# Projection, value, turn-out and output side work of the first attention, divided into halves behind two units in a row

## The chip, the cores and the metric

The kernel runs on one core of one Trainium2 chip. The metric is device time in microseconds (us) of one execution, and the number compared is the median of several runs. A core has five engines that run their own instruction lists side by side and meet at semaphores: TensorE (PE in the profile, with its weight loads as PEld), VectorE (DVE), ScalarE (ACT), GpSimd (POOL) and SyncE (SP), which here issues DMAs.

## The reference, cut to what matters

The input x has shape (4, 512, 256). Four stages add to it in turn: a cross-attention of 16 heads of 64 over a context with a mask, a mixture of experts with 8 experts, a banded self-query attention, and a second mixture of experts. The change touches the first stage alone:

```
Qh = (layernorm(x) @ Wq).reshape(n, t, 16, 64)      # Wq, Wk, Wv: 256 x 1024
Kh = (ctx @ Wk).reshape(n, t, 16, 64)
Vh = (ctx @ Wv).reshape(n, t, 16, 64)
energy = einsum('nqhd,nkhd->nhqk', Qh, Kh) / 8
energy = where(mask == 0, -1e20, energy)
heads_out = einsum('nhqk,nkhd->nqhd', softmax(energy), Vh)
x = x + heads_out.reshape(n, t, 1024) @ Wo          # Wo: 1024 x 256
```

## The kernel before, in words

Every float32 matrix is held as two float16 parts, hi and lo, and a product is made of three matmuls (`three_products`, L197 to L199).

The first attention runs over 32 groups, numbered g = 0 to 31: 4 batches of 8 pairs of heads. A group has 8 units, numbered j = 0 to 7: two heads times four blocks of 128 queries. A unit u is a row of steps on several engines, and TensorE takes them with lags: in its step u it makes the scores of unit u (`score`, L427 and L428, into one of two banks `sc`), transposes the exponentials of unit u-3 (`turn`, L435, into `et`) and multiplies the values of unit u-5 (`attend`, twelve small matmuls into `ob`). VectorE does the masking and the minimum of unit u (L540, L542), then the lo part of unit u-3 (L518). ScalarE does the hi part of unit u-3 (L484), then the exponential of unit u (L491).

Behind its step u TensorE does a piece of side work, which `side_work(g, j)` names. In the kernel before these are whole pieces:

- j = 0: `k`, six matmuls of 512 columns, the keys of group g+1;
- j = 1: `q`, six such matmuls, the queries of group g+1;
- j = 4: `v`, six such matmuls, values of the next batch (batches 0 to 2 only, so groups 0 to 23);
- j = 5: `w`, 24 matmuls of 256 columns, an output projection of the batch before (in groups 9 to 12, 17 to 20 and 25 to 28);
- j = 7: `t`, four transposes of the normalised output of group g-1.

All of them write into one of two PSUM banks `pj`, taken in turn. `open_group` makes the first matmul of a piece wait until the piece two before it has been taken out of its bank: by ScalarE (`copy`, L478, semaphore `copied`) or, for `w`, by VectorE (`add_out`, L514, semaphore `added`). ScalarE does the copy of a piece of step u-1 as the last thing of its step u, and VectorE does `add_out` of a `w` of step u-1 behind its L518 of step u.

After the copy GpSimd splits the piece into hi and lo (`split`, L333 and L335; for k and q into `nat_k` and `nat_q`), in the order in which the pieces are finished. In twelve groups (0 to 3, 8 to 11, 16 to 19) it also turns a block of the mask into a bias (`bias`, L310) between q and v. SyncE then moves the keys and queries to the layout of the scores with DMAs (`stack(g+1)`: four of `kk`, L288, four of `qq`, L292), and behind these it loads the next mask block (L279). The first score of group g+1 waits until the `kk` and `qq` of its first head have landed, the first two of each four (semaphore `stacked[0]`).

Of the kernel before, what the change touches and what calls it, by code (L numbers as in the profile page):

```python
# [17 lines left out]
B, S, D = 4, 512, 256  # L18
NT = B * S // P
QT = S // P  # L20
DT = D // P
# [3 lines left out]
CT = CW // P  # L25
PAIRS = HEADS // 2
# [175 lines left out]
def side_work(g, j):  # L202


    p, b = g % PAIRS, g // PAIRS
    if j == 0 and g + 1 < PAIRS0:
        return "k", g + 1
    if j == 1 and g + 1 < PAIRS0:
        return "q", g + 1
    if j == 4 and b + 1 < B:  # L210
        return "v", (b + 1, p)
    if j == 5 and b >= 1 and 1 <= p <= QT:
        return "w", (b - 1, p - 1)
    if j == 7 and g >= 1:
        return "t", g - 1
    return None


def number_groups():

    groups, copies, adds = {}, {}, {}
    order = [("k", 0), ("q", 0)] + [("v", (0, n)) for n in range(V_GROUPS)]
    order += [side_work(g, j) for g in range(PAIRS0) for j in range(UNITS) if side_work(g, j) is not None]
# [11 lines left out]
def phase_attention0(nc, sem, T, dram):  # L235
# [3 lines left out]
    with ExitStack() as ctx:  # L239
# [32 lines left out]
        with nc.Block() as block:  # L272
# [31 lines left out]
            @block.gpsimd  # L304
            def _(pool):
                def bias(n):
                    pool.wait_ge(mask_in[n % 2], 16 * (n // 2 + 1))
                    if n >= 2 * QT:
                        pool.wait_ge(masked_ok, (n // QT - 1) * PAIRS * UNITS)
                    pool.tensor_scalar(mask_bias[n // QT % 2][:, n % QT, :], mask_raw[n % 2][:], 0.0, MASKED, ALU.is_equal, ALU.mult).then_inc(bias_ok, 1)  # L310

                def split(what):
                    kind, at = what
                    n = COPY0[what]
                    src = raw[n % NRAW][:]
                    pool.wait_ge(copied, n + 1)
                    if kind == "v":
                        b, part = at
                        if b >= 2:
                            pool.wait_ge(pv_done, (b - 1) * PAIRS * UNITS)  # L320
                        hi, lo = v_part(v[b % 2].hi, part), v_part(v[b % 2].lo, part)
                        src = src.rearrange("p (h d) -> p h d", d=DK)
                    elif kind == "t":
                        b, ct = at // PAIRS, at % PAIRS
                        if b >= 2:
                            pool.wait_ge(pj_full, GROUP0["w", (b - 2, QT - 1)] + 1)
                        hi, lo = o_t[b % 2].hi[:, ct, :], o_t[b % 2].lo[:, ct, :]
# [12 lines left out]
                bias(0)  # L340
                bias(1)
                split(("k", 0))
                split(("q", 0))
                bias(2)
                bias(3)
                for n in range(V_GROUPS):
                    split(("v", (0, n)))
                for g in range(PAIRS0):
                    for j in range(UNITS):
                        what = side_work(g, j)  # L350
                        if what in COPY0:
                            split(what)
                        if j == 2 and g // PAIRS + 1 < B and g % PAIRS < QT:
                            bias((g // PAIRS + 1) * QT + g % PAIRS)
                split(("t", PAIRS0 - 1))

            @block.tensor
            def _(pe):
# [7 lines left out]
                            pe.wait_ge(added, ADD0[before] + 1)  # L366
                    return pj[n % 2]

                def project(what, w, src_t):

                    out = open_group(what)
                    b, col = what[1] // PAIRS, (what[1] % PAIRS) * P
                    for c in range(DT):
                        mm = three_products(pe, out[:], (w.hi[:, c, col:col + P], w.lo[:, c, col:col + P]),
                                            (src_t.hi[:, c, b * S:(b + 1) * S], src_t.lo[:, c, b * S:(b + 1) * S]),
                                            c == 0, c == DT - 1)
                    mm.then_inc(pj_full, 1)

                def project_v(what):
# [3 lines left out]
                    out = open_group(what)  # L383
                    for c in range(DT):
                        mm = three_products(pe, out[:], (T.ctx_t.hi[:, c, rows], T.ctx_t.lo[:, c, rows]),
                                            (T.wv0.hi[:, c, cols], T.wv0.lo[:, c, cols]), c == 0, c == DT - 1)
                    mm.then_inc(pj_full, 1)

                def turn_out(what):
                    g = what[1]  # L390
# [6 lines left out]
                def project_out(what):  # L397
                    b, qt = what[1]
                    out = open_group(what)
                    pe.wait_ge(split_done, COPY0["t", (b + 1) * PAIRS - 1] + 1)  # L400
                    cols = slice(qt * P, (qt + 1) * P)
                    for ct in range(CT):
                        mm = three_products(pe, out[:, 0:D], (o_t[b % 2].hi[:, ct, cols], o_t[b % 2].lo[:, ct, cols]),
                                            (T.wo0.hi[:, ct, :], T.wo0.lo[:, ct, :]), ct == 0, ct == CT - 1)
                    mm.then_inc(pj_full, 1)

                def do_side_work(what):
                    if what[0] == "k":
                        project(what, T.wk0, T.ctx_t)
                    elif what[0] == "q":  # L410
                        project(what, T.wq0, T.z_t)
                    elif what[0] == "v":
                        project_v(what)
                    elif what[0] == "t":
                        turn_out(what)
                    else:
                        project_out(what)

                def score(u):
                    g, j = u // UNITS, u % UNITS  # L420
# [30 lines left out]
                project(("k", 0), T.wk0, T.ctx_t)  # L451
                project(("q", 0), T.wq0, T.z_t)
                for n in range(V_GROUPS):
                    project_v(("v", (0, n)))
                pe.wait_ge(v_const, 4)
                units = PAIRS0 * UNITS
                for u in range(units + ATTEND_LAG):
                    if u < units:
                        score(u)
                    if 0 <= u - TURN_LAG < units:  # L460
                        turn(u - TURN_LAG)
                    if u >= ATTEND_LAG:
                        attend(u - ATTEND_LAG)
                    what = side_work(u // UNITS, u % UNITS) if u < units else None
                    if what is not None:
                        do_side_work(what)
                turn_out(("t", PAIRS0 - 1))
                for qt in range(QT):
                    project_out(("w", (B - 1, qt)))

            @block.scalar
            def _(act):
# [25 lines left out]
                for u in range(units + TURN_LAG):  # L498
                    if u >= TURN_LAG:
                        turned_part(u - TURN_LAG)  # L500
                    if u < units:
                        exponent(u)
                    what = side_work((u - 1) // UNITS, (u - 1) % UNITS) if 1 <= u <= units else None
                    if what in COPY0:
                        copy(what)
                copy(("t", PAIRS0 - 1))

            @block.vector
            def _(dve):
# [36 lines left out]
                for u in range(units + TURN_LAG):  # L546
# [1351 lines left out]
```

## Time and profile before

| | us |
|---|---|
| runs | 1392.19, 1393.86, 1393.17; median 1393.17 |
| profiled execution, its own time | 1389.44 |
| its span, first to last instruction | 1387.7 |
| TensorE, matmuls | 1127.9 busy (81%) |
| VectorE | 799.5 (58%) |
| ScalarE | 626.4 (45%) |
| GpSimd | 507.8 (37%) |
| granted TensorE clock over the span | 0.905 |

The first attention fills the span from about 72 us (first score) to 573 us. Busy time of matmuls counts each from its start to its modelled end, and neighbours overlap. So the pace of TensorE is read from start to start: two score matmuls of a unit start 0.21 to 0.22 us apart though each is listed with 0.38. A timeline row gives the start, the duration, the engine, the line, the operation, and at its end, in brackets, the idle time of the engine before it with what released it. A row of the windows view gives the stretch, its length, the busy time (and in parentheses the number of instructions) of PE, PEld, DVE, ACT and POOL, then the granted clock as a share of 2.4 GHz, the busy share of the DMA engines and GB/s.

### The profile page before, as it was taken

How to read it: one execution, taken by the hardware profiler on the slowest of the kernel's cores; microseconds unless marked ns; L12 is line 12 of the kernel's file. 1: busy time of each engine (PE TensorE's matmuls, PEld its weight loads, DVE VectorE, ACT ScalarE, POOL GpSimd, SP SyncE). 2: the span in 40 equal slices, each digit the busy share in tenths (PEclk: the TensorE clock that was granted, in tenths of full speed). 3: DMA queues.
4: the chain of work that ended last, by engine and by line, in shares of the span. 5: the costliest groups of instructions: out<-in, count | busy, mean ns of one | idle time of the engine just before them, and what ended most of it. 6: DMA issues, size and time to landing. Idle time of an engine off the chain costs nothing. (4 is left out here: it accounts for less than half of the span.)

```text
span 1387.7 us, 29963 instructions
## 1 busy us (share of the span) xinstructions
PE 1127.9 (81%) x10895; PEld 856.4 (62%) x10896; DVE 799.5 (58%) x2325; ACT 626.4 (45%) x1171; POOL 507.8 (37%) x491
## 2 busy tenths in 40 slices
PE   2499999999999999454799916558899953699997
PEld 1166777777777776353588812335666633588886
DVE  7267787787778778546511134356677751255553
ACT  3277787787778778010022113125455530333331
POOL 2666545444544332210325332189820003011112
PEclk9899999999999999655599967979999985799998
DMA  6122222222222121430146342545521141111110
GB/s 242 53 62 62 70 55 63 55 70 62 63 50 67 48 50 44 151 124 1 31 129 204 108 113 88 178 130 165 161 64 44 33 127 65 47 32 27 26 23 9
DMA packets 80222, 110.94 MB, mean 80 GB/s; under 512 B 11552, under 2 KB 58400, under 8 KB 79712
## 3 DMA queue, kind: packets, MB, share of 16 engines
q1 hardware_dynamic: 69632, 88.23, 21.6%
q0 software_dynamic: 10464, 21.01, 6.4%
q8 instruction: 81, 1.33, 0.4%
q14 instruction: 45, 0.37, 0.1%
HBM read 59.86 MB, written 24.70 MB: 61 GB/s over the span
## 5 line engine op out<-in xcount | busy, mean ns | idle before, releaser
L542 DVE CUSTOM_DVE_ANT_0 masked<-sc,mask_bias 128x512 f32<-128x512 f32 x256 | 175.5, 686 | 57.7 <-issue 39.3
L518 DVE TENSOR_TENSOR e_t_lo<-et,e_t_hi 128x512 f16<-128x512 f32 x256 | 176.6, 690 | 49.9 <-ACT e_t_hi L484 47.6
L491 ACT ACTIVATE e<-masked,neg_max 128x512 f32<-128x512 f32 x256 | 184.3, 720 | 26.9 <-DVE neg_max L542 26.4
L484 ACT ACTIVATE e_t_hi<-et 128x512 f16<-128x512 f32 x256 | 152.1, 594 | 88.1 <-PE et L435 87.8
L435 PEld LDWEIGHTS et<-ident,e 128*128 128x128 f32 x1024 | 125.7, 141 | 54.1 <-ACT e L491 6.3
L435 PE MATMUL et<-ident,e 128*128 128x128 f32 x1024 | 154.1, 273 | 1.4 <-ACT e L491 0.7
L1266 ACT ACTIVATE d_e<-d_st 128x384 f32<-128x384 f32 (+1 forms) x192 | 98.0, 529 | 113.4 <-PE d_st L1351 98.1
L197 PE MATMUL ob<-v_hi,e_t_hi 128*128 128x65 f16 x1024 | 119.0, 193 | 0.6 <-DVE e_t_lo L518 0.6
L198 PE MATMUL ob<-v_lo,e_t_hi 128*128 128x65 f16 x1024 | 119.2, 193 | 0.0
L199 PE MATMUL ob<-v_hi,e_t_lo 128*128 128x65 f16 x1024 | 118.4, 193 | 0.0
L427 PE MATMUL sc<-kk,qq 128*128 128x512 f16 x256 | 96.9, 379 | 5.2 <-DMA qq<-nat_q 4.8
L197 PE MATMUL h_hb<-h_xt_hi,experts_hi 128*128 128x256 f16 x352 | 97.1, 276 | 4.3 <-DVE h_xt_lo L1732 3.9
L198 PE MATMUL h_hb<-h_xt_lo,experts_hi 128*128 128x256 f16 x352 | 97.0, 276 | 0.0
L199 PE MATMUL h_hb<-h_xt_hi,experts_lo 128*128 128x256 f16 x352 | 97.0, 275 | 0.0
L428 PE MATMUL sc<-kk,qq 128*128 128x512 f16 x256 | 96.9, 379 | 0.0
L198 PEld LDWEIGHTS ob<-v_lo,e_t_hi 128*128 128x128 f16 x1024 | 94.5, 97 | 2.9
L197 PEld LDWEIGHTS ob<-v_hi,e_t_hi 128*128 128x128 f16 x1024 | 95.7, 97 | 0.8 <-DVE e_t_lo L518 0.7
L1703 POOL DMA_INDIRECT out<-h_res,h_token x22 | 34.2, 1553 | 166.8 <-DVE h_res L1755 161.5
L199 PEld LDWEIGHTS ob<-v_hi,e_t_lo 128*128 128x128 f16 x1024 | 94.7, 97 | 0.0
L1346 PE MATMUL d_wk<-d_k,d_q 128*128 128x384 f16 (+1 forms) x256 | 72.4, 310 | 26.2 <-DMA d_q<-d_k 22.7
L478 ACT ACTIVATE raw<-pj 128x512 f32<-128x512 f32 x128 | 75.0, 586 | 32.0 <-POOL v_lo L335 15.9
L1278 DVE TENSOR_REDUCE d_mx<-d_wk 128x1 f32<-128x384 f32 x128 | 66.9, 553 | 35.0 <-PE d_wk L1351 28.7
(315 smaller groups left out, 2902.2 us busy)
## 6 DMA issues: line engine op xcount, KB each, us to landing
kk<-nat_k SPq DMA_DIRECT2D x128, 128.0 KB, 2.3
raw<-in_fc SPq DMA_DIRECT2D x16, 1024.0 KB, 6.7
qq<-nat_q SPq DMA_DIRECT2D x128, 64.0 KB, 2.0
mask_raw<-in_mask SPq DMA_DIRECT2D x16, 256.0 KB, 2.9
scratch_stack<-c_qk_hi SPq DMA_DIRECT2D x32, 128.0 KB
scratch_stack<-c_qk_lo SPq DMA_DIRECT2D x32, 128.0 KB
d_expert_raw<-in_gate_w POOLq DMA_DIRECT2D x8, 512.0 KB, 4.1
d_expert_raw<-in_up_w POOLq DMA_DIRECT2D x8, 512.0 KB, 4.0
```

Of the source, the lines that this page charges most:

```text
L197: pe.matmul(out, stat[0], mov[0], start=first, stop=False)
L198: pe.matmul(out, stat[0], mov[1], start=False, stop=False)
L199: return pe.matmul(out, stat[1], mov[0], start=False, stop=last)
L427: pe.matmul(sc[j % 2][:], stat, kk[g % 2][:, a, 0, :], start=True, stop=False)
L428: pe.matmul(sc[j % 2][:], stat, kk[g % 2][:, a, 1, :], start=False, stop=True).then_inc(scores, 1)
L435: mm = pe.transpose(et[u % 2][:, kt, :], e[u % NBUF][:, kt * P:(kt + 1) * P], T.ident[:])
L478: nc.scalar.activation(raw[n % NRAW][:], pj[GROUP0[what] % 2][:], ACT.Copy).then_inc(copied, 1)
L484: nc.scalar.activation(e_t[u % NBUF].hi[:], et[u % 2][:], ACT.Copy).then_inc(turned_hi, 1)
L491: nc.scalar.activation(e[u % NBUF][:], masked[u % NBUF][:], ACT.Exp, bias=neg_max[:, g % 2, j:j + 1], scale=-1.0).then_inc(exp_ok, 1)
L518: nc.vector.tensor_tensor(e_t[u % NBUF].lo[:], et[u % 2][:], e_t[u % NBUF].hi[:], ALU.subtract).then_inc(turned_lo, 1)
L542: nc.vector.tensor_tensor_reduce(masked[u % NBUF][:], sc[j % 2][:], mask_bias[g // PAIRS % 2][:, j % QT, :], -SCALE0, 3e38, ALU.add, ALU.m ...
L1266: nc.scalar.activation(part(e[m % EBUF][:, 2 * half + i // 3, :, :], i % 3), src, ACT.Exp, scale=SCALE1).then_inc(exp_ok, 1)
```

## The change: what it does, and the diff

`side_work` now returns a list of halves. The keys stand behind units 0 and 1, the queries behind 2 and 3, the values behind 4 and 5, the output projection behind 6 and 7, and the turn-out stays behind 7. A half of k, q or v is three matmuls; a half of w is twelve. Both halves add into the same bank, only the first half opens it, and only the second half reports it full. A new function `complete(u)` lists the pieces that end behind unit u, and ScalarE, VectorE and GpSimd follow it: they take a piece out one step after its second half. Matmuls, copies, splits and DMAs are the same in number and size.

```diff
     p, b = g % PAIRS, g // PAIRS
-    if j == 0 and g + 1 < PAIRS0:
-        return "k", g + 1
-    if j == 1 and g + 1 < PAIRS0:
-        return "q", g + 1
-    if j == 4 and b + 1 < B:
-        return "v", (b + 1, p)
-    if j == 5 and b >= 1 and 1 <= p <= QT:
-        return "w", (b - 1, p - 1)
+    parts = []
+    if j < 2 and g + 1 < PAIRS0:
+        parts.append((("k", g + 1), j))
+    if 2 <= j < 4 and g + 1 < PAIRS0:
+        parts.append((("q", g + 1), j - 2))
+    if 4 <= j < 6 and b + 1 < B:
+        parts.append((("v", (b + 1, p)), j - 4))
+    if j >= 6 and b >= 1 and 1 <= p <= QT:
+        parts.append((("w", (b - 1, p - 1)), j - 6))
     if j == 7 and g >= 1:
-        return "t", g - 1
-    return None
+        parts.append((("t", g - 1), 1))
+    return parts
+
+
+def complete(u):
+
+    return [what for what, half in side_work(u // UNITS, u % UNITS) if half == 1] if 0 <= u < PAIRS0 * UNITS else []
...
# POOL: the order of the splits, and the place of the mask bias
-                        if j == 2 and g // PAIRS + 1 < B and g % PAIRS < QT:
+                        if j == 4 and g // PAIRS + 1 < B and g % PAIRS < QT:
                             bias((g // PAIRS + 1) * QT + g % PAIRS)
...
# PE: one half of a projection (project_v and project_out alike)
-                def project(what, w, src_t):
+                def project(what, w, src_t, halves):
 
-                    out = open_group(what)
+                    out = open_group(what) if 0 in halves else pj[GROUP0[what] % 2]
                     b, col = what[1] // PAIRS, (what[1] % PAIRS) * P
-                    for c in range(DT):
+                    for c in halves:
...
-                    mm.then_inc(pj_full, 1)
+                    if 1 in halves:
+                        mm.then_inc(pj_full, 1)
...
# ACT
-                    what = side_work((u - 1) // UNITS, (u - 1) % UNITS) if 1 <= u <= units else None
-                    if what in COPY0:
-                        copy(what)
+                    for what in complete(u - 1):
+                        if what in COPY0:
+                            copy(what)
...
# DVE
-                        what = side_work((u - 1) // UNITS, (u - 1) % UNITS) if u >= 1 else None
-                        if what in ADD0:
-                            add_out(what)
+                        for what in complete(u - 1):
+                            if what in ADD0:
+                                add_out(what)
```

The instruction lists of GpSimd and SyncE keep their order. Two places on other engines move.

On ScalarE, in a group with v, from the copy of t to that of q, before: L484 is the hi part (`e_t_hi`), L491 the exponential (`e`), L478 the copy out of `pj`.

```order
L478 ACTIVATE raw<-pj 128x512 [waits split_done,pj_full]
L484 ACTIVATE e_t_hi<-et 128x512 [waits pv_done,turned]
L491 ACTIVATE e<-masked,neg_max 128x512 [waits turned,masked_ok]
L478 ACTIVATE raw<-pj 128x512 [waits split_done,pj_full]
L484 ACTIVATE e_t_hi<-et 128x512 [waits pv_done,turned]
L491 ACTIVATE e<-masked,neg_max 128x512 [waits turned,masked_ok]
L478 ACTIVATE raw<-pj 128x512 [waits split_done,pj_full]
```

In the changed kernel, from the copy of t to that of k (its L487, L493 and L500 are L478, L484 and L491 of before):

```order
L487 ACTIVATE raw<-pj 128x512 [waits split_done,pj_full]
L493 ACTIVATE e_t_hi<-et 128x512 [waits pv_done,turned]
L500 ACTIVATE e<-masked,neg_max 128x512 [waits turned,masked_ok]
L493 ACTIVATE e_t_hi<-et 128x512 [waits pv_done,turned]
L500 ACTIVATE e<-masked,neg_max 128x512 [waits turned,masked_ok]
L487 ACTIVATE raw<-pj 128x512 [waits split_done,pj_full]
```

Before, the copies of t, k and q stood in three steps in a row (j = 0, 1, 2); now k's is two steps behind t's, and q's two behind k's, in step j = 4.

On VectorE in group 9, around the addition of the output projection (`x<-pj,x`), before; it stands between the lo part of step j = 6 and the masking of step j = 7, and behind it a whole step follows before TensorE opens the bank again:

```order
L527 RECIPROCAL rden<-ob 128x4 [waits normed,pv_done]
L529 TENSOR_TENSOR o<-ob,rden 128x4x64 [waits rden_ok]
L540 MEMSET gate 1x1 [waits exp_ok,scores]
L542 ISA masked,neg_max<-sc,mask_bias 128x512
L542 ISA neg_max 128x1
L518 TENSOR_TENSOR e_t_lo<-et,e_t_hi 128x512 [waits turned_hi]
L514 TENSOR_TENSOR x<-pj,x 128x256 [waits pj_full]
```

And in the changed kernel, where the addition stands in step j = 0 of group 10 (L523, L527, L551, L536 and L538 are L514, L518, L542, L527 and L529 of before):

```order
L549 MEMSET gate 1x1 [waits exp_ok,scores]
L551 ISA masked,neg_max<-sc,mask_bias 128x512
L551 ISA neg_max 128x1
L527 TENSOR_TENSOR e_t_lo<-et,e_t_hi 128x512 [waits turned_hi]
L523 TENSOR_TENSOR x<-pj,x 128x256 [waits pj_full]
L549 MEMSET gate 1x1 [waits exp_ok,scores]
L551 ISA masked,neg_max<-sc,mask_bias 128x512
L551 ISA neg_max 128x1
L527 TENSOR_TENSOR e_t_lo<-et,e_t_hi 128x512 [waits turned_hi]
L536 RECIPROCAL rden<-ob 128x4 [waits normed,pj_full,pv_done]
```

The addition moved two steps back, over the border of the group. The first matmul of k in step j = 0 is the one that waits for it (`added`), in both kernels.

## Rows read from the trace of the kernel before

**Rows 1.** Two stretches of the first attention, busy time by engine, from the windows view.
```profile
100.00:200.00 100.00, 97.19 (x1127) 70.45 (x1126) 78.26 (x243) 78.17 (x136) 54.53 (x59) 1.00 0.26 62
300.00:400.00 100.00, 100.00 (x1138) 74.85 (x1137) 73.67 (x230) 72.62 (x127) 52.40 (x56) 1.00 0.24 60
```

**Rows 2.** Waits from 72 to 560 us: engine, line, releaser, us, times, longest.
```profile
PE sc L427 <- DMA qq<-nat_q: 4.8, 4, 2.0
```

**Rows 3.** Timeline of TensorE in group 15: unit starts, q's first matmul, group 16.
```profile
297.67 0.38 PE L427 MATMUL sc<-kk,qq 128*128 128x512 f16 x1
...
300.19 0.38 PE L427 MATMUL sc<-kk,qq 128*128 128x512 f16 x1
...
301.42 0.38 PE L197 MATMUL pj<-z_t_hi,wq_hi 128*128 128x512 f16 x1
...
302.72 0.38 PE L427 MATMUL sc<-kk,qq 128*128 128x512 f16 x1
...
305.18 0.38 PE L427 MATMUL sc<-kk,qq 128*128 128x512 f16 x1
...
311.85 0.38 PE L427 MATMUL sc<-kk,qq 128*128 128x512 f16 x1
```

**Rows 4.** Timeline, the way of q(16) from its bank: copy, split, DMA issue.
```profile
304.89 0.59 ACT L478 ACTIVATE raw<-pj 128x512 f32<-128x512 f32 x1
...
306.24 1.16 POOL L335 TENSOR_TENSOR nat_q<-raw,nat_q 128x512 f16<-128x512 f32 x1
...
307.42 2.44 SPq L292 DMA_DIRECT2D qq<-nat_q  x4
```

**Rows 5.** Timeline of groups 3 and 4: SyncE, the delayed group start, GpSimd, SyncE again.
```profile
127.31 2.51 SPq L292 DMA_DIRECT2D qq<-nat_q  x4
129.87 0.58 SPq L279 DMA_DIRECT2D mask_raw<-in_mask  x1
129.99 0.39 PE L427 MATMUL sc<-kk,qq 128*128 128x512 f16 x1 [0.88 <-DMA qq<-nat_q]
...
132.76 1.94 POOL L310 TENSOR_SCALAR mask_bias<-mask_raw 128x512 bf16<-128x512 int32 x1 [6.12 <-DMA mask_raw<-in_mask]
...
142.52 2.53 SPq L292 DMA_DIRECT2D qq<-nat_q  x4
```

**Rows 6.** Timeline of group 18, step j = 6: score, lo part, addition.
```profile
356.76 0.38 PE L427 MATMUL sc<-kk,qq 128*128 128x512 f16 x1
...
358.46 0.69 DVE L518 TENSOR_TENSOR e_t_lo<-et,e_t_hi 128x512 f16<-128x512 f32 x1 [0.36 <-ACT e_t_hi L484]
...
359.07 0.41 DVE L514 TENSOR_TENSOR x<-pj,x 128x256 f32<-128x256 f32 x1
```

**Rows 7.** Timeline of TensorE: first scores of groups 24, 25, 29, 30, 31.
```profile
435.91 0.38 PE L427 MATMUL sc<-kk,qq 128*128 128x512 f16 x1
...
449.33 0.39 PE L427 MATMUL sc<-kk,qq 128*128 128x512 f16 x1 [0.20 <-DVE e_t_lo L518]
...
511.55 0.38 PE L427 MATMUL sc<-kk,qq 128*128 128x512 f16 x1
...
524.60 0.38 PE L427 MATMUL sc<-kk,qq 128*128 128x512 f16 x1
...
537.73 0.38 PE L427 MATMUL sc<-kk,qq 128*128 128x512 f16 x1
```

**Rows 8.** Timeline of SyncE in group 5: the second of the four issues of qq(6).
```profile
155.91 1.87 SPq L292 DMA_DIRECT2D qq<-nat_q  x1
```

**Rows 9.** Timeline of TensorE: first scores of groups 1 and 2.
```profile
85.08 0.39 PE L427 MATMUL sc<-kk,qq 128*128 128x512 f16 x1 [1.96 <-DMA qq<-nat_q]
...
99.28 0.38 PE L427 MATMUL sc<-kk,qq 128*128 128x512 f16 x1
```

**Rows 10.** Windows view: around the wait of group 1, and the end of the attention.
```profile
85.00:100.00 15.00, 14.92 (x171) 10.96 (x172) 10.99 (x36) 10.42 (x20) 7.06 (x7) 1.00 0.36 86
...
560.00:565.00 5.00, 5.00 (x26) 3.46 (x24) 0.26 (x1) 0.00 (x0) 0.00 (x0) 0.51 0.01 3
```

More of the change, by code:

```diff
@@ L222, in number_groups @@
     order = [("k", 0), ("q", 0)] + [("v", (0, n)) for n in range(V_GROUPS)]
-    order += [side_work(g, j) for g in range(PAIRS0) for j in range(UNITS) if side_work(g, j) is not None]
+    order += [what for u in range(PAIRS0 * UNITS) for what in complete(u)]
     order += [("t", PAIRS0 - 1)] + [("w", (B - 1, qt)) for qt in range(QT)]
@@ L349, in _ @@
                     for j in range(UNITS):
-                        what = side_work(g, j)
-                        if what in COPY0:
-                            split(what)
-                        if j == 2 and g // PAIRS + 1 < B and g % PAIRS < QT:
+                        for what in complete(g * UNITS + j):
+                            if what in COPY0:
+                                split(what)
+                        if j == 4 and g // PAIRS + 1 < B and g % PAIRS < QT:
                             bias((g // PAIRS + 1) * QT + g % PAIRS)
@@ L376, in project, with project_v @@
                                             c == 0, c == DT - 1)
-                    mm.then_inc(pj_full, 1)
-                def project_v(what):
+                    if 1 in halves:
+                        mm.then_inc(pj_full, 1)
+                def project_v(what, halves):
                     b, n = what[1]
@@ L382, in project_v @@
                     cols = slice((n % 2) * 512, (n % 2 + 1) * 512)
-                    out = open_group(what)
-                    for c in range(DT):
+                    out = open_group(what) if 0 in halves else pj[GROUP0[what] % 2]
+                    for c in halves:
                         mm = three_products(pe, out[:], (T.ctx_t.hi[:, c, rows], T.ctx_t.lo[:, c, rows]),
                                             (T.wv0.hi[:, c, cols], T.wv0.lo[:, c, cols]), c == 0, c == DT - 1)
-                    mm.then_inc(pj_full, 1)
+                    if 1 in halves:
+                        mm.then_inc(pj_full, 1)
                 def turn_out(what):
@@ L395, in turn_out, with project_out, do_side_work @@
                     mm.then_inc(pj_full, 1)
-                def project_out(what):
+                def project_out(what, halves):
                     b, qt = what[1]
-                    out = open_group(what)
+                    out = open_group(what) if 0 in halves else pj[GROUP0[what] % 2]
                     pe.wait_ge(split_done, COPY0["t", (b + 1) * PAIRS - 1] + 1)
                     cols = slice(qt * P, (qt + 1) * P)
-                    for ct in range(CT):
+                    for ct in [half * CT // 2 + i for half in halves for i in range(CT // 2)]:
                         mm = three_products(pe, out[:, 0:D], (o_t[b % 2].hi[:, ct, cols], o_t[b % 2].lo[:, ct, cols]),
                                             (T.wo0.hi[:, ct, :], T.wo0.lo[:, ct, :]), ct == 0, ct == CT - 1)
-                    mm.then_inc(pj_full, 1)
-                def do_side_work(what):
+                    if 1 in halves:
+                        mm.then_inc(pj_full, 1)
+                def do_side_work(what, half):
                     if what[0] == "k":
-                        project(what, T.wk0, T.ctx_t)
+                        project(what, T.wk0, T.ctx_t, [half])
                     elif what[0] == "q":
-                        project(what, T.wq0, T.z_t)
+                        project(what, T.wq0, T.z_t, [half])
                     elif what[0] == "v":
-                        project_v(what)
+                        project_v(what, [half])
                     elif what[0] == "t":
@@ L416, in do_side_work @@
                     else:
-                        project_out(what)
+                        project_out(what, [half])
                 def score(u):
@@ L449, in attend @@
                     mm.then_inc(pv_done, 1)
-                project(("k", 0), T.wk0, T.ctx_t)
-                project(("q", 0), T.wq0, T.z_t)
+                project(("k", 0), T.wk0, T.ctx_t, [0, 1])
+                project(("q", 0), T.wq0, T.z_t, [0, 1])
                 for n in range(V_GROUPS):
-                    project_v(("v", (0, n)))
+                    project_v(("v", (0, n)), [0, 1])
                 pe.wait_ge(v_const, 4)
@@ L463, in _ @@
                         attend(u - ATTEND_LAG)
-                    what = side_work(u // UNITS, u % UNITS) if u < units else None
-                    if what is not None:
-                        do_side_work(what)
+                    if u < units:
+                        for what, half in side_work(u // UNITS, u % UNITS):
+                            do_side_work(what, half)
                 turn_out(("t", PAIRS0 - 1))
                 for qt in range(QT):
-                    project_out(("w", (B - 1, qt)))
+                    project_out(("w", (B - 1, qt)), [0, 1])
             @block.scalar
@@ L502, in _ @@
                         exponent(u)
-                    what = side_work((u - 1) // UNITS, (u - 1) % UNITS) if 1 <= u <= units else None
-                    if what in COPY0:
-                        copy(what)
+                    for what in complete(u - 1):
+                        if what in COPY0:
+                            copy(what)
                 copy(("t", PAIRS0 - 1))
```

## The prediction

> **What bounds the kernel now.** I read the windows first. In the first attention TensorE is busy 97.19 of 100 us early on and 100.00 of 100 in the middle, at a granted clock of 1.00, while VectorE, ScalarE and GpSimd have 74 to 78, 73 to 78 and 52 to 55 [rows 1]. So TensorE sets the pace, and an engine with a quarter of its time free can only matter through a wait. The list of waits comes next: TensorE's matmuls wait longest for the `qq` DMAs, 4.8 us in four places of the whole stage [rows 2]. Side work moved about on an engine that never waits costs nothing and gains nothing; only waits that go or come count. To price these I took the starts of the score matmuls in the timeline, since a matmul's listed duration overlaps its neighbour's. Group 15 stands for the groups with k, q and v and no w: it runs from 297.67 to 311.85, which is 14.18 us. Its first unit (with k) takes 2.52 and its second (with q) 2.53, so q is complete at 302.72, 5.05 us into the group; four units have passed at 305.18, 7.51 us into it [rows 3].
>
> How much slack has each result of the side work? The way of q(16) is the longest: complete on TensorE at 302.72, copied by ScalarE at 304.89, split on GpSimd with the lo part from 306.24, and issued by SyncE at 307.42, that is 4.70 us after completion [rows 3, 4]. The copy starts 2.17 us late because it stands behind the exponential of the next step, which has to wait for that step's score. I looked at all 31 such ways: in 22 of them the time is 4.70 to 4.72 us, and in the nine others, which follow a mask block or the first values, it is longer. What an issue needs until the score may start is read where TensorE waited for it: issue at 127.31, score at 129.99, so 2.68 us [rows 5]. In group 15 there were 311.85 - 307.42 = 4.43 us, so q had 1.75 us to spare.
>
> **The change part by part.** The work is unchanged, instruction by instruction; every term is a wait.
>
> *Keys, queries and the start of the next group.* k ends one unit later and q two. The first four units hold the same matmuls as before, so q is complete 7.51 us into the group in place of 5.05: 2.46 us later, against 1.75 to spare. The ScalarE place of q's copy relative to the next step's score and exponential is the same as before, so I keep 4.70. The next group then can't start before 7.51 + 4.70 + 2.68 = 14.89 us: 0.71 us more than 14.18. GpSimd is free when q's copy comes, since k was split well before. This falls on each group that has v and no w and isn't already held by something else: 5 to 8, 13 to 16 and 21 to 23, eleven of them, 7.8 us. In the twelve groups 9 to 12, 17 to 20 and, with less room, 25 to 28, w makes the group 16.8 (15.55 in the last batch) us long, more than 14.89: nothing.
>
> *Last batch.* Without v the groups are shorter: group 24 takes 449.33 - 435.91 = 13.42, group 29 13.05, group 30 13.13 [rows 7]. Each becomes 14.89: 1.47 + 1.84 + 1.76 = 5.1 us. TensorE idles about 2 us in each. A wait of 1.96 us before group 1 left the granted clock at 1.00 in the 15 us behind it [rows 9, 10], so I add nothing for the clock.
>
> [...]
>
> *First batch.* Groups 1 to 4 hang on a ring of GpSimd and SyncE: the mask load is issued behind qq, the bias waits for it, v, t, k and q wait behind the bias on GpSimd, and the next qq waits for these. One turn is 142.52 - 127.31 = 15.21 us [rows 5], longer than 14.89, and the order on both engines is unchanged, so the ring keeps its pace. It only enters later: group 2 starts 0.71 us later than 85.08 + 14.20 = 99.28 [rows 9], and the first mask load with it. Between 0.7 and 1.4 us, since in groups 1 to 3 the time from the mask's issue to the bias varies by 0.7 us: I take 1.0. Group 1 itself is held by the splits of the first values, which the change doesn't touch: nothing.
>
> *Output projection and its bank.* This is the largest term. Pieces take the two banks in turn, in the order k, q, v, w, t; k of the next group so takes the bank of w. Before, w ended in step 5 and was added in step 6, two steps ahead of that k. Now it ends in step 7, and its addition stands behind VectorE's masking and lo part of the next group's step 0, both of which need TensorE's own work of that step. In step 6 of group 18 the score starts at 356.76, the lo part at 358.46 and the addition at 359.07 for 0.41: done 2.72 us after the score [rows 6]. k's first matmul is due when q's was in its step: 301.42 - 300.19 = 1.23 us after the score [rows 3]. TensorE so waits 2.72 - 1.23 = 1.5 us. Nothing on TensorE may pass this matmul: the next score stands behind it, and VectorE, ScalarE and GpSimd behind that. It happens behind each of the twelve w: 12 x 1.5 = 18.0 us. It can't be hidden by the q term, since it lies ahead of q in the same group and delays it as well; in groups 13, 21 and 29 both are paid. Bounds: from 0, if VectorE came to it in time, to 12 x 2.72 = 33, if the score itself were held; the row is the same sequence of instructions, so 18.0.
>
> *SyncE's long issues.* The second qq issue of group 6 starts at 155.91 and lasts 1.87 [rows 8], in place of 0.60; by the next issue that is 1.64 us lost. Seven of the 31 second issues are like it, by 0.8 to 1.6 us, in the stacks of groups 6, 9, 13, 15, 22, 27 and 29. Today the slack of q hides them. That slack is gone. If the same instructions are slow again (SyncE's list is unchanged), those of 6, 9, 15 and 22 count in full, 1.64 + 0.80 + 0.78 + 1.09 = 4.3, and 27 and 29 with what exceeds the group of 15.55 us, 0.8 + 0.4. Together 5.5 us; if they fall elsewhere, 0 to 6. I take 5.5.
>
> *v, t and the end.* v is complete one unit later and is needed a batch later, t has not moved: nothing. In group 31, which has no k, q or v, VectorE was behind before; after a wait of 2 us it starts even. I take 0.7 us back (bounds 0 and 1.5).
>
> Sum: 7.8 + 5.1 + 1.0 + 18.0 + 5.5 - 0.7 = 36.7 us. On the profiled execution's own 1389.44 that is 1426.1; the median of the runs lies 3.7 higher, 1393.17, and so the forecast is 1429.9, rounded to **1430 us**.
>
> **The rivals.**
>
> *A. Half of it.* Only one of the two waits is real: VectorE reaches the addition early, or q comes through in less than 4.70 us because ScalarE is less pressed. Without the first: 1430 - 18 = 1412. Without the q terms (7.8, 5.1, 1.0 and 5.5): 1411. Against the first: the addition can't precede the lo part, which can't precede the turn of the same step. Against the second: 4.70 is the same in groups of different load, so it is a chain of latencies and no queue.
>
> *B. No change.* TensorE is full, the same matmuls run, all moved waits find cover: 1393. For it speaks [rows 1], and against it the 1.75 us of slack, which is less than the 2.46 us by which q moves.
>
> *C. Faster.* In one mechanism: even units keep VectorE and ScalarE from falling behind TensorE, so the small waits of the last batch and the waits of group starts go. Its place is groups 24 and 29 to 31 (the first three 13.42, 13.05 and 13.13 us [rows 7], against two units of 2.53, five of 1.23 and one of 1.70 with t, 12.9: 0.9 us, and about 1.4 in group 31) and the starts of groups 1 to 4 (5.3 us in rows of the timeline, the largest 1.96 [rows 9]). It would give at most 7.6 us, 1385.6. It decides if q's way from its bank to the landing is under 14.18 - 7.51 = 6.67 us; the rows make it 7.38.
>
> *D. The clock falls as well.* At the end of the attention, behind sparse work with a wait in it, the granted clock is 0.51 in a stretch of 5 us, the level of 1.2 GHz [rows 10]. Against it stands the wait of 1.96 us that left it alone [rows 9]. If the new waits brought such a stretch, say two of 5 us at half speed, 5 us more: 1435; in many places 1440.
>
> **How the numbers follow.** Forecast as summed 0.72, A 0.11, B 0.03, C 0.02, D 0.12. The range reaches down to A's 1412, which also holds the sum with the long issues at 0 and a w wait of 0.5 us less, and up to D in many places, 1440; B and C are left out. A difference within 0.2% (2.8 us) can't be told from none. Faster 0.03 (C and a remnant), same 0.03 (B), slower 0.94.
>
> **What would show it.** In the changed profile the first score of groups 6 to 9, 14 to 17 and 22 to 24 waits for the `qq` DMA, with some 0.7 us (2 us in 25, 30 and 31), group lengths of 14.9 in place of 14.2. TensorE's first k matmul behind each w waits for the addition (its L523), 1.5 us, twelve times. GpSimd and SyncE keep their busy time; everything behind the attention is merely later by the sum. I am wrong in the main term if that k matmul doesn't wait, and in the second if q's issue comes less than 12 us into the group.

## The result, and the profile after

| | before | changed |
|---|---|---|
| median of the runs, us | 1392.68 (4 runs, 1388.98 to 1393.86) | 1425.44 (4 runs, 1422.51 to 1429.8) |
| profiled execution, us | 1389.44 | 1425.6 |
| its span, us | 1387.7 | 1423.9 |

The ratio is 1.0251, with a 95% interval of 1.022 to 1.0283 (here and below the ratio is an estimate from the single runs and need not be the quotient of the two medians, which is 1.0235 here). The changed kernel is slower, by 32.8 us between the medians and by 36.2 between the two profiled executions. The forecast was 1430, in a range of 1412 to 1440.

The windows of the changed kernel, the same two stretches as in [rows 1]:

```profile
100.00:200.00 100.00, 92.11 (x1061) 66.28 (x1062) 76.33 (x231) 74.67 (x128) 51.14 (x55) 1.00 0.24 58
300.00:400.00 100.00, 94.53 (x1084) 70.04 (x1083) 73.16 (x221) 70.96 (x122) 49.63 (x53) 1.00 0.24 59
```

TensorE was busy 97.19 and 100.00 of 100; now it stands still for 8 and 5.5. The list of waits from 72 to 600 us says for what (in [rows 2] the first row had 4 times and 4.8 us, and the second didn't exist):

```profile
PE sc L436 <- DMA qq<-nat_q: 20.1, 19, 3.2
PE pj L197 <- DVE x L523: 16.6, 12, 1.4
```

The first group of waits, in group 14 of the changed kernel (its first score; the first score of unit 4, which follows q's last matmul; the copy, split and issue of q; the first score of group 15), against [rows 3] and [rows 4]:

```profile
297.44 0.39 PE L436 MATMUL sc<-kk,qq 128*128 128x512 f16 x1 [0.83 <-DMA qq<-nat_q]
...
304.96 0.38 PE L436 MATMUL sc<-kk,qq 128*128 128x512 f16 x1
...
307.13 0.59 ACT L487 ACTIVATE raw<-pj 128x512 f32<-128x512 f32 x1
...
308.48 1.16 POOL L341 TENSOR_TENSOR nat_q<-raw,nat_q 128x512 f16<-128x512 f32 x1
309.66 2.39 SPq L298 DMA_DIRECT2D qq<-nat_q  x4
312.21 0.39 PE L436 MATMUL sc<-kk,qq 128*128 128x512 f16 x1 [0.39 <-DMA qq<-nat_q]
```

q is complete 7.52 us into the group, issued 4.70 us later, and the next group starts 2.55 us behind the issue: 14.77 us in all, where the group took 14.20 before. The copy still starts 2.17 us after q's completion.

The second group of waits, at the start of group 11, with VectorE's masking, lo part and addition of w, against [rows 6]:

```profile
244.02 0.38 PE L436 MATMUL sc<-kk,qq 128*128 128x512 f16 x1
...
244.66 0.69 DVE L551 CUSTOM_DVE_ANT_0 masked<-sc,mask_bias 128x512 f32<-128x512 f32 x1 [1.23 <-issue]
...
245.72 0.69 DVE L527 TENSOR_TENSOR e_t_lo<-et,e_t_hi 128x512 f16<-128x512 f32 x1 [0.36 <-ACT e_t_hi L493]
246.33 0.41 DVE L523 TENSOR_TENSOR x<-pj,x 128x256 f32<-128x256 f32 x1
...
246.80 0.39 PE L197 MATMUL pj<-ctx_t_hi,wk_hi 128*128 128x512 f16 x1 [1.38 <-DVE x L523]
```

VectorE has been idle for 1.23 us and takes the masking first, because it stands first in its list, although w was complete before the score at 244.02. The addition ends at 246.74, 2.72 us behind the score, and k starts at 246.80 instead of 245.25.

The difference of the two profiled executions, by lengths of groups (first score to first score). "Groups behind a w" are those whose k waits for the addition: 10 to 13, 18 to 21 and 26 to 29. Group 11, for one, has a w of its own as well.

| term | forecast | measured | from |
|---|---|---|---|
| w's bank, 12 groups behind a w | 18.0 | 18.2 | 18.35 in place of 16.83 us, 1.52 each |
| q's way, 11 groups with v and no w | 7.8 | 6.3 | 14.77 in place of 14.20, 0.57 each |
| last batch, groups 24, 29, 30 | 5.1 | 4.7 | 14.77 in place of 13.42, 13.05, 13.13 |
| first batch, groups 1 to 4 | 1.0 | 1.1 | start of group 5, less a long issue of 1.55 |
| SyncE's long issues | 5.5 | 5.6 | what groups 4, 5, 7, 13, 16 and 30 have over the others: 1.55, 0.57, 1.35, 0.45, 0.12, 1.54 |
| group 31 and all behind it | -0.7 | 0.3 | 36.2 less the rest |
| sum | 36.7 | 36.2 | |

The last row is small beside what a single execution can show: from the first score of group 31 to the end, the twelve profiled executions of this document take 845.6 to 853.8 us, though no edit touches anything there.

One stretch at half clock came as well. It is the level of 1.2 GHz, from 573.4 to 576.8, in the windows of the changed kernel:

```profile
560.00:573.00 13.00, 10.40 (x135) 7.75 (x133) 10.16 (x31) 9.49 (x17) 5.31 (x6) 1.00 0.24 57
573.00:577.00 4.00, 3.39 (x22) 2.40 (x23) 1.39 (x4) 1.46 (x3) 0.00 (x0) 0.57 0.07 17
```

It comes with the end of TensorE's longest wait of the stage, 3.2 us before group 31. The first unit of that group took 2.36 us in place of 1.30.

### The profile page after: what moved, and what is told of

It is laid out like the page before. It is cut to its first block and busy times, and to the rows that moved or that the text cites. A ratio compares the mean times of both kernels' runs of the same rounds, so it can differ in the third digit from the quotient of the medians.

```text
span 1423.9 us, 29963 instructions
## 1 busy us (share of the span) xinstructions
PE 1130.7 (79%) x10895; PEld 857.2 (60%) x10896; DVE 809.7 (57%) x2325; ACT 631.5 (44%) x1171; POOL 508.0 (36%) x491
## 5 line engine op out<-in xcount | busy, mean ns | idle before, releaser
L527 DVE TENSOR_TENSOR e_t_lo<-et,e_t_hi 128x512 f16<-128x512 f32 x256 | 177.0, 692 | 69.7 <-ACT e_t_hi L493 68.4
L493 ACT ACTIVATE e_t_hi<-et 128x512 f16<-128x512 f32 x256 | 152.6, 596 | 135.5 <-PE et L444 134.8
L551 DVE CUSTOM_DVE_ANT_0 masked<-sc,mask_bias 128x512 f32<-128x512 f32 x256 | 175.6, 686 | 61.4 <-issue 40.1
L500 ACT ACTIVATE e<-masked,neg_max 128x512 f32<-128x512 f32 x256 | 183.3, 716 | 10.5 <-DVE neg_max L551 7.7
L487 ACT ACTIVATE raw<-pj 128x512 f32<-128x512 f32 x128 | 74.8, 584 | 32.7 <-POOL v_lo L341 14.0
```

The source lines that it names most:

```text
L487: nc.scalar.activation(raw[n % NRAW][:], pj[GROUP0[what] % 2][:], ACT.Copy).then_inc(copied, 1)
L493: nc.scalar.activation(e_t[u % NBUF].hi[:], et[u % 2][:], ACT.Copy).then_inc(turned_hi, 1)
L500: nc.scalar.activation(e[u % NBUF][:], masked[u % NBUF][:], ACT.Exp, bias=neg_max[:, g % 2, j:j + 1], scale=-1.0).then_inc(exp_ok, 1)
L527: nc.vector.tensor_tensor(e_t[u % NBUF].lo[:], et[u % 2][:], e_t[u % NBUF].hi[:], ALU.subtract).then_inc(turned_lo, 1)
L551: nc.vector.tensor_tensor_reduce(masked[u % NBUF][:], sc[j % 2][:], mask_bias[g // PAIRS % 2][:, j % QT, :], -SCALE0, 3e38, ALU.add, ALU.m ...
```

## The experiments

The theory was that two waits, each with its own cause, make up the cost and add up, and the rivals were that one hides the other, that the even spacing costs or gains something in itself, and that another wait takes the place of the one removed. Unless said otherwise each edit is made on the changed kernel. The kernel before was run again beside the experiments: its median is 1391.29 us for e1 to e4, 1390.5 for e5 to e8 and 1389.84 for e9 and e10.

**e1: the addition at the head of VectorE's step.**

```diff
                     if u < units:
+                        for what in complete(u - 1):
+                            if what in ADD0:
+                                add_out(what)
+                    if u < units:
                         maximum(u)
                     if u >= TURN_LAG:
                         turned_part(u - TURN_LAG)
                     if u < units:
-                        for what in complete(u - 1):
-                            if what in ADD0:
-                                add_out(what)
```

> The changed kernel, with VectorE's addition of w moved to the head of its step u, ahead of the masking of that step; nothing else. Theory (the 12 waits of TensorE's k matmul are VectorE's order: the addition stands behind two operations that need TensorE's next step): all twelve waits of 1.38 us go, the groups behind a w shrink from 18.35 to 16.83 us, and the time falls by 12 x 1.51 = 18 us, to about 1407. The waits for the qq DMAs stay (about 17 us over the kernel before). Rival (the late bank only stands in front of another wait, such as the masking or the copies of ScalarE, which takes its place): the k matmul waits for something else and the time stays at 1420 to 1426.

Measured: 1407.76 us, ratio 1.0126 (1.008 to 1.0172). The list of waits has no row from the addition to TensorE any more. In the timeline of this run, at the start of group 11:

```profile
240.91 0.42 DVE L523 TENSOR_TENSOR x<-pj,x 128x256 f32<-128x256 f32 x1 [0.36 <-PE pj L199]
...
241.79 0.69 DVE L551 CUSTOM_DVE_ANT_0 masked<-sc,mask_bias 128x512 f32<-128x512 f32 x1 [0.45 <-issue]
```

```profile
241.15 0.38 PE L436 MATMUL sc<-kk,qq 128*128 128x512 f16 x1
...
242.38 0.38 PE L197 MATMUL pj<-ctx_t_hi,wk_hi 128*128 128x512 f16 x1
```

The addition ends 1.05 us before k is due. The masking starts 0.64 us behind the score, as before, so the early addition costs it nothing. The groups 10 to 12 and 18 to 20 take 16.8 us. The cause is the place in VectorE's list. The theory's 18 us are 17.7 between the medians (1425.44 was measured on another occasion, with its own runs of before); in the profiles group 31 starts 18.8 us earlier than in the changed kernel.

**e2: k and q whole again.**

```diff
     if j < 2 and g + 1 < PAIRS0:
-        parts.append((("k", g + 1), j))
-    if 2 <= j < 4 and g + 1 < PAIRS0:
-        parts.append((("q", g + 1), j - 2))
+        parts += [(("kq"[j], g + 1), 0), (("kq"[j], g + 1), 1)]
```

> The changed kernel with k whole behind unit 0 and q whole behind unit 1, as in the kernel before; v, w and t as in the changed kernel. Theory (the two costs are separate and add up): the waits for the qq DMAs go back to those of the kernel before, 17 us are gained, the twelve waits of the k matmul of 1.4 to 1.5 us stay, and the time is about 18 us over the kernel before, 1410 to 1412. Rival (the q term was small and w's is nearly all of it): 1420 or more. Rival (both waits overlap, so that undoing one uncovers the other): 1418 to 1425.

Measured: 1412.49 us, ratio 1.0141 (1.0089 to 1.0192), half a microsecond over the theory's range and outside the ranges of both rivals. Its waits are those of the kernel before for the DMAs and those of the changed kernel for the bank:

```profile
PE pj L197 <- DVE x L521: 16.6, 12, 1.4
PE sc L434 <- DMA qq<-nat_q: 5.8, 5, 2.2
```

So the two costs are separate. Undoing one leaves the other whole: group 31 starts 35.9 us later in the changed kernel than in the kernel before, and 17.1 us later in e1 and 19.7 in e2, which is 36.8 together.

**e3: both edits.**

> Both edits at once: k and q whole behind units 0 and 1, and VectorE's addition of w at the head of its step; v and w stay in halves behind units 4, 5 and 6, 7. Theory: no term is left, so the time is that of the kernel before within 2.8 us, 1390 to 1395. Rival (halves cost something in themselves, by the banks being open longer or by the clock): some 3 to 10 us over the kernel before.

Measured: 1390.39 us, ratio 1.0007 (0.9974 to 1.0039). v and w in halves cost nothing. All groups but the first five have the length of before within 0.04 us, except group 24 with 13.77 in place of 13.42.

**e4: the dose, q one unit later and not two** (with e1's edit):

```diff
-    if 2 <= j < 4 and g + 1 < PAIRS0:
-        parts.append((("q", g + 1), j - 2))
+    if 1 <= j < 3 and g + 1 < PAIRS0:
+        parts.append((("q", g + 1), j - 1))
```

> The dose: k in halves behind units 0 and 1, q in halves behind units 1 and 2, so q is complete one unit later than in the kernel before and not two; VectorE's addition at the head of its step, so w's wait is out of the way. Theory (a threshold: q's way of 4.70 us to the issue and 2.55 us to the landing, against the length of the group): q is complete after 1.88 + 2.52 + 1.88 = 6.28 us, the next group could start after 13.53, which is under 14.20; only groups 29 and 30 pay, 0.4 to 0.5 us each, and a long issue of SyncE about 0.8: 1 to 3 us over the kernel before, 1393 to 1396. Rival (cost grows in proportion with the shift of q): half of the 17 us, 1401.

Measured: 1401.75 us, ratio 1.0061 (1.0036 to 1.0087), which is a miss of the theory's number and the number of the rival. The groups decide between them. Undisturbed ones take 14.22 to 14.24 us against 14.20, where half of the changed kernel's cost would make 14.48; so cost is not in proportion to the shift. But they have no slack, where 0.7 us were expected. GpSimd and SyncE in group 6 of this run, which starts at 162.41:

```profile
171.53 0.61 POOL L339 CAST nat_q<-raw 128x512 f16<-128x512 f32 x1
172.22 1.17 POOL L341 TENSOR_TENSOR nat_q<-raw,nat_q 128x512 f16<-128x512 f32 x1
```

```profile
171.53 2.39 SPq L294 DMA_DIRECT2D kk<-nat_k  x4
173.96 2.51 SPq L298 DMA_DIRECT2D qq<-nat_q  x4
```

q's split ends at 173.39, 10.98 us into the group, as computed. SyncE issues the four kk until 173.92 and only then the first qq: 0.57 us lost, because k, and not q, had moved to the limit. The expectation had followed q's way and forgotten who stands ahead of it in SyncE's queue. Without slack the long issues show: groups 5, 7, 8, 14, 16 and 23 took 14.8 to 15.5 us, 5.5 more together. Groups 24, 29 and 30 took 14.2 in place of 13.1 to 13.4, which is 3.1, and groups 1 to 4 together cost 2.6. By group 31 this run is 10.5 us behind the kernel before, as its median is.

**e5: the kernel before, mask blocks loaded ahead of the stack.**

```diff
                 for g in range(PAIRS0 - 1):
-                    stack(g + 1)
                     if g // PAIRS + 1 < B and g % PAIRS < QT:
                         load_mask((g // PAIRS + 1) * QT + g % PAIRS)
+                    stack(g + 1)
```

> The kernel before (whole pieces) with one edit on SyncE: each mask block is loaded ahead of the stack of its group and not behind it. Theory (groups 2 to 4 are held by a ring: qq issue, mask load, bias, v, t, k and q splits, kk and qq issues, 15.2 us a turn): with the mask landed early the turn has no DMA in it and is under 14.2 us, the waits before groups 3, 4 and 5 (1.27, 1.04 and 1.02 us) go, and the time is 3.3 us under the kernel before, a ratio of 0.9976. Rival (these groups are held by GpSimd's work and not by the load): groups 2 to 4 keep 15.2 us and the ratio is 1.000.

Measured: 1388.09 us, ratio 0.9979 (0.9954 to 1.0004). The interval touches 1, so by the time alone it isn't shown faster. The profile is clear: the first scores of groups 1 to 5.

```profile
85.00 0.39 PE L427 MATMUL sc<-kk,qq 128*128 128x512 f16 x1 [0.69 <-DMA qq<-nat_q]
...
99.19 0.38 PE L427 MATMUL sc<-kk,qq 128*128 128x512 f16 x1
...
113.40 0.38 PE L427 MATMUL sc<-kk,qq 128*128 128x512 f16 x1
...
127.59 0.38 PE L427 MATMUL sc<-kk,qq 128*128 128x512 f16 x1
...
141.80 0.38 PE L427 MATMUL sc<-kk,qq 128*128 128x512 f16 x1
```

The groups are 14.2 us apart and wait for nothing but in the first row; against 145.21 before, group 5 starts 3.4 us earlier, and every later group keeps these 3.4 us. So the ring of [rows 5] was real, and the DMA in it was the mask load.

**e6: e4, with kk and qq issued head by head.**

```diff
                         for half in range(2):
                             sp.dma_start(kk[i][...], nat["k"][...]).then_inc(stacked[a], 16)
-                    sp.wait_ge(split_done, COPY0["q", g] + 1)
-                    for a in range(2):
+                        if a == 0:
+                            sp.wait_ge(split_done, COPY0["q", g] + 1)
                         for half in range(2):
                             sp.dma_start(qq[i][...], nat["q"][...]).then_inc(stacked[a], 16)
```

> The run with q one unit later and the early addition (e4), with one more edit on SyncE: the four kk and four qq DMAs go head by head (kk, kk, qq, qq of the first head, then of the second). Theory (in e4 the next group was held by SyncE still issuing kk, complete at 4.41 + 4.70 + 2.45 us for k, when q was ready, which made 14.2 us without any slack): the first qq can be issued when q is split, 10.98 us into the group, the next group could start at 13.53, the long issues are covered again, groups 24, 29 and 30 shrink from 14.2 to 13.5, and the time is 1 to 3 us over the kernel before. Rival (q's own way was longer than 4.70 in e4): group lengths and time stay as in e4, a ratio of 1.006.

Measured: 1395.48 us against 1390.5, ratio 1.004 (1.0016 to 1.0064). The time is a miss, 5.0 us over before and not 1 to 3. The part on kk held: groups 24 and 29 shrink to 13.58 us, against 13.53 computed (group 30 took 14.95), and groups 6 and 8 to 22 are back at 14.2 or 16.8, but for group 18 with 17.03. But groups 1 to 5 take 15.7 to 17.1 us, more than the 14.2 to 15.5 of the kernel before: the ring now has one more pair of issues behind q's split (kk of the second head), and the mask load waits behind all of them. From mask load to mask load it takes 15.7 to 15.9 us, where a turn was 15.2. In group 5 there is also a stretch at half clock, behind a wait of 2.7 us. By group 6 the run was 5.8 us behind the kernel before, and 8.6 by group 30. So what was missed is mostly the ring; e9 checks this by taking the mask load out of it.

**e7: the kernel before with both edits on SyncE.**

> The kernel before with both SyncE edits: mask blocks loaded ahead of the stack, and kk and qq issued head by head. No side work is moved. Theory: the early waits go as in the run with the early mask, and the second edit adds slack that nothing needs there, so it is 3.3 to 4.5 us under the kernel before (with some part of the wait before group 1), a ratio near 0.997. Rival: the second head's keys, now issued behind the first head's queries, come late for unit 4: they have four units, 7.5 us, so nothing is expected of it.

Measured: 1388.25 us, ratio 0.9973 (0.9953 to 0.9993). By the ratio this one beats the kernel before, if only just: by 0.27%, and by 2.3 us between the medians. Its groups are those of e5 within 0.2 us, and group 5 starts 3.7 us earlier than in the kernel before. What the second edit adds to e5 is too small to be told.

**e8: the changed kernel profiled again.**

> The changed kernel as it is, profiled a second time, for SyncE's long issues (1.4 to 2.0 us in place of 0.6). If they belong to certain instructions, they fall in the same stacks as in the first profile (before groups 5, 6, 8, 14 and 31 by the group starts) and the group lengths are the same within 0.1 us. If they come by time or by chance, they fall in other stacks, and about as many of them, 12 to 15, are found. The time is 1420 to 1430 in either case, with the same twelve waits of 1.38 us behind w.

Measured: 1426.58 us, one run. Four issues of kk or qq mostly take 2.4 to 2.55 us together. Those over 2.75 were 14 in the first profile of the changed kernel and 13 here, and 12 of them are the same stacks: for instance those of q for groups 5 and 8, in the first profile

```profile
143.86 3.87 SPq L298 DMA_DIRECT2D qq<-nat_q  x4
...
190.22 3.72 SPq L298 DMA_DIRECT2D qq<-nat_q  x4
```

and in the second:

```profile
144.53 3.28 SPq L298 DMA_DIRECT2D qq<-nat_q  x4
...
190.75 3.29 SPq L298 DMA_DIRECT2D qq<-nat_q  x4
```

Between these two profiles of one kernel they are tied to places, while their size varies by some 0.6 us, and with it group lengths (group 4 took 16.77 and 16.53, group 30 16.31 and 15.91), so the part on lengths within 0.1 us failed. Between kernels with the same SyncE list they move: the kernel before had q's for 6, 9, 11, 13, 15, 20, 22, 24, 25, 27 and 29, of which the changed kernel shares 27 alone (and kk's for 18). The other profiles say what moves them. The kernels with k and q whole (before, e2, e3, e5; 12 to 14 long stacks each) share 8 to 11 with each other; those with q behind units 2 and 3 (changed, e1, e8, e10; 12 to 14) share 9 to 12; across the two sorts it is 0 to 3. So the places go with where k and q stand, and not with w's place or VectorE's order.

**e9: halves with every wait repaired** (e6 with the mask load of e5).

> Halves everywhere with all four repairs: k behind units 0 and 1, q behind 1 and 2, VectorE's addition at the head of its step, kk and qq head by head, and mask blocks loaded ahead of the stack (the last of these is new against e6). Theory (what is left in e6 is the ring of mask load, GpSimd and SyncE in groups 1 to 5, 15.7 to 15.8 us a turn): these groups go to 14.2 us, and the time is that of the kernel before with the early mask (e5, e7) within 2 us, a ratio of 0.998 to 0.999. So halves neither cost nor gain anything once no result is late. Rival (even units give TensorE something of their own): 3 us or more under e7, 0.995 or less. Rival (q's later issue still binds the early groups): as e6, 1.004.

Measured: 1391.27 us against 1389.84, ratio 1.0007 (0.9983 to 1.003), a little over the range that the theory gave (and 3 us over e5 and e7, not 2), with that range partly inside the interval. The rival of a gain by even spacing is out: its 0.995 lies below the interval. All groups from 1 to 22 take 14.2 to 14.3 or 16.8 us, so the ring is gone (the time is 1.4 us over the kernel before, where e6 had 5.0), and group 5 starts 3.6 us earlier than before; group 23 met a long issue (15.51), groups 24, 29 and 30 take 13.6, and by group 31 the gain is 1.5 us.

**e10: one number of the change, w behind units 5 and 6.**

```diff
-    if j >= 6 and b >= 1 and 1 <= p <= QT:
-        parts.append((("w", (b - 1, p - 1)), j - 6))
+    if 5 <= j < 7 and b >= 1 and 1 <= p <= QT:
+        parts.append((("w", (b - 1, p - 1)), j - 5))
```

> The changed kernel with one number moved: the halves of w behind units 5 and 6 and not 6 and 7; VectorE's order is as in the changed kernel. Theory (the k matmul waits only because the addition falls into its own step): the addition is done 2.72 us after the score of step 7, and k is due 1.70 + 1.23 = 2.93 us after it, so all twelve waits of 1.38 us go by a margin of 0.2 us; 12 x 1.51 = 18 us less than the changed kernel, about 1407. Rival (w in two halves is slow to come out whatever its place): the k matmul still waits, over 1 us each, 1420 or more.

Measured: 1409.09 us against 1389.84, ratio 1.0134 (1.0084 to 1.0185). None of the twelve k matmuls waits, and groups 10 to 12 and 18 to 20 take 16.8 us. e1 moved the addition, e10 moved w, and either removes the wait; so it is the distance between the two that costs.

## Why the prediction was right, step by step

- **TensorE bounds the stage, so only waits count.** Right. e3 (v and w in halves) and e9 (all in halves) equal the kernel before within their intervals.
- **w and its bank, 12 x 1.5 us.** Right in place, number and size (1.52), shown by e1 and e10 from two sides.
- **q's way against the group's length.** Right in mechanism: completion to issue was 4.70 again, in a group with another spacing. The term that was off is the last one, from issue to start: 2.55 and not 2.68, so 14.77 us and not 14.89. The row it came from was one of a group with a mask load behind it, where the first two qq issues, which the score waits for, took 1.24 us (all four 2.51); in the undisturbed groups of the changed kernel they took 1.10 (2.39). That makes 0.14 us in each of 11 groups, the 1.5 us between 7.8 and 6.3, and 0.4 in the last batch.
- **The ring of the first batch.** Right: groups 1 to 3 took 15.2 to 15.4 us in the changed kernel, and e5 shows the ring, since the edit that takes the mask load out of it frees the early groups.
- **SyncE's long issues.** The sum was right (5.6 against 5.5), and its reasoning was not. The step "if the same instructions are slow again" failed: of the six stacks named only that of group 6 cost anything (0.57), and the stacks of groups 5, 8 and 31, not named, cost 1.55, 1.35 and 1.54 us. The other step, to count the length of the second issue as the loss, failed as well. The score waits for the landing, and the landing can be late though both issues are short. So it is before group 31, where of the four issues only the last was long (all issues of the stack; the first two alone, with the time from issue to landing; the score):

```profile
569.52 3.25 SPq L298 DMA_DIRECT2D qq<-nat_q  x4
...
L298 SPq DMA_DIRECT2D qq<-nat_q x2: 461/529/597, 569.5 to 570.0; - x2
...
DMA to landing us min/median/max: 1.9/2.7/3.5
...
573.61 0.61 PE L436 MATMUL sc<-kk,qq 128*128 128x512 f16 x1 [3.21 <-DMA qq<-nat_q]
```

The second DMA landed 3.5 us behind its issue and not 2.0. In the kernel before, the stacks of groups 11, 20, 24 and 25 were like this (a long third or fourth issue, the second DMA landing 0.9 to 1.4 us late), and the prediction's count of seven left them out. For group 25 the landing came 0.05 us ahead of the first score, so the 13.42 us of group 24 in [rows 7] probably held such a wait already. What did hold is that there are as many late stacks as before, and that with the slack gone some of them show. That the two sums agree is luck.
- **The end.** Forecast 0.7 back, measured 0.3 more. The 0.7 was right by itself: in e10, which waits 1.7 us before group 31 and keeps its clock, the first seven units of that group take 9.32 us in place of 10.09. In the changed kernel they took 10.48, since the clock fell behind the longest wait, the mechanism of rival D in one place; by e10 it cost 1.2 us.
- **The forecast against the median.** 1430 lies 4.6 us over 1425.44, while for the profiled execution the sum was 1426.1 against 1425.6. Most of this is that the profiled execution of before was 3.7 under the median I added it to, which the sum took for a lasting difference.
- **Rivals.** A fell (both waits are there), B and C fell (the groups that C named, 24 and 29 to 31, got longer). D came true in one place here, and in one place each in e1, e6, e8 and e10, at 0.9 to 1.7 us each, where the rival had put 2.5 on a stretch.

## What to carry to other kernels

When a producer's piece is spread out, compute when each *result* is complete, and follow it through every in-order list between it and its next user: here ScalarE's step, SyncE's queue and VectorE's step. On the saturated TensorE of this stage evenness was worth nothing (e9), and slack was: 1.75 us per group covered both the way of q and the irregular landings of its DMAs. If a release (an addition, a copy out of a bank) can stand first in its step at no cost, put it there.

## What the runs showed of the hardware that wasn't expected

- One in about five stacks of four DMA issues took 2.8 to 4.2 us instead of the usual 2.4 to 2.55, in each of the nine profiles in which the kk and the qq stand together (12 to 15 of 64), at the same places in two profiles of one kernel (12 of 13), and at others when k and q stand elsewhere on TensorE. With it DMAs land late that were issued before the long issue. So the wait may lie in the transfers and the long issue be its sign; what causes it was not tested and stays open.
- Waits of TensorE of 3.2 us (changed kernel and e1), 2.8 (e8), 2.7 (e6) and 2.5 (e10) each came with a stretch of 3.4 us at a granted clock of 0.5, which began between 0.2 us before and 0.9 us behind the end of the wait. The eighteen other waits for qq of the changed kernel, of up to 2.4 us, did not.
- Behind the first attention, where nothing was edited, single profiled executions differ by up to 8 us, so e4, e6 and e9 are read by their group lengths; a gain under 3 us needed twelve timed executions to leave the interval just below 1 (e7).
